# A spiking feed-forward layer with routed experts: ScalarE's bound check on x moved behind the third group's GELU, and more warming products in TensorE's waits

## Chip, cores, metric

The kernel runs on one NeuronCore of a Trainium2 chip. The metric is the device time of one execution in microseconds (us); lower is better. Engines are called PE (TensorE, with PEld for its weight loads), DVE (VectorE), ACT (ScalarE), POOL (GpSimd) and SP (SyncE).

## What is computed

```python
# x: (32, 64, 256) f32, cond: (32, 256) f32, router_w (8, 256), w1 (8, 256, 1024), w2 (8, 1024, 256)
rates  = relu(x) * 0.001
c      = cond[:, None, :] + cumsum(rates, axis=1)
spikes = (floor(c) - floor(c one step before)) / 0.001         # mostly zero
probs  = softmax(spikes.reshape(2048, 256) @ router_w.T)       # 8 experts
top_v, top_i = top_k(probs, 2);  top_v /= sum(top_v)           # capacity 640 slots an expert
for k in range(2):                                              # expert e of token t, if it fits
    out[t] += top_v[t, k] * (gelu(spikes[t] @ w1[e]) @ w2[e])
result = x + out
```

## The kernel before

The kernel counts on few spikes: at most 256 rows of the 2,048 have one, and each has a single spiking channel. It first runs through x, then works out a short list of active rows, routes them, fetches for each row and expert the one row of w1 that its spike picks, and adds the few changed rows to the output. If one of these assumptions fails, a verdict at the end starts a slow general path that does not run here.

**First stage (about 4.7 to 16 us).** x comes in eight groups of 128 x 512. For each, ACT and DVE split the rates in two terms, PE sums them over time (L543, L546, L551), and the floors go through PE once more (L562).

**The middle (16 to 31 us).** It is one chain of small steps that hop between PE, DVE, ACT and POOL: find the spikes, list the rows, compute logits (L621), choose two experts (L1023), rank (L630), drop what exceeds capacity (`limit` L860, `limit_c` L1029, `kept` L1032, `routed` L1033), place (L638 to L649), make one-hot lanes (`ev_lane`, L1044) and, in `make_map(d)` (L662), the list of w1 rows for each of four groups d of two experts. `make_index(d)` writes `w1_index`, and POOL's indirect DMA (L501) gathers 128 rows of w1 into `w1_got`.

**The groups (31 to 56 us).** For each group d: `hidden(d)` (L687) is 8 f32 products, in two halves of four; `gelu(d)` on ACT (L846) takes each half as it is ready; `project(d)` (L703) is 16 products on half the array's columns each; `take_y` (DVE, L1061) and `round_y` (ACT, L877) read the result; `combine(d)` (L713 to L720) adds it to the output rows. PE's order is written out by hand: hidden 0, project 0, take_pairs (L674), hidden 1, hidden 2, project 1, combine 0, hidden 3, project 2, combine 1, project 3, combine 2, combine 3, verdict.

**Warming products.** `keep_warm(n)` issues n matmuls of 512 bf16 columns (L532) whose result nobody reads. They stand in PE's own queue, ahead of the matmuls that come next, so one that is still running when the next input arrives delays it. Six places in the middle take `WARM_MID[0..5]` of them: behind the last `weigh`; behind the event offsets (L589); behind the list and level products (L595 to L603); behind the logits (L621); behind the ranks (L630, L632); behind the places (L638 to L649). Four more, one behind each `make_map(d)`, take `WARM[d]`; the last stands right ahead of `hidden(0)`.

**The check of x.** ACT reads all of x once (128 x 4096), with a bound subtracted, and accumulates whatever is above into column 0 of `faults` (L871); `x_seen` tells DVE. It stands between a dummy activation that loads the GELU table (L867) and `gelu(0)`. DVE waits for `x_seen` ahead of `take_y(1)` and reduces `faults` to one number behind `rest_y(1)` (L1146, L1147), which the verdict matmul at the very end needs.

```python
WARM = (3, 3, 3, 3)
WARM_MID = (2, 2, 2, 1, 1, 2)
```

Of the kernel before, what the change touches and what calls it, by code (L numbers as in the profile page):

```python
# [12 lines left out]
ACT = mybir.ActivationFunctionType  # L13
# [12 lines left out]
def adaln_ffn_kernel(nc, x, cond, router_w, w1, w2, out):  # L26
    B, T, H = x.shape
    E, _, FFN = w1.shape
    N = B * T
    TILES = N // P  # L30
# [16 lines left out]
    FINE = 2.0 ** -17  # L47
    X_MAX = RUN_MAX / (T * float(DT)) - 0.05
    WARM_START = 8
    WARM = (3, 3, 3, 3)  # L50
    WARM_MID = (2, 2, 2, 1, 1, 2)
    XG = TILES // 2
    SIGN_GROUPS = (1, 3, 5, 6)
    PLAIN_GROUPS = tuple(g for g in range(XG) if g not in SIGN_GROUPS)
# [8 lines left out]
    with ExitStack() as ctx:  # L63
        def sb(name, shape, dt=F32):
            return ctx.enter_context(nc.sbuf_tensor(name, shape, dt))
# [4 lines left out]
        def sem(name):  # L70
            return ctx.enter_context(nc.semaphore(name))
# [38 lines left out]
        x_sb = sb("x_sb", [P, TILES, H])  # L110
# [8 lines left out]
        x_bound = sb("x_bound", [P, 1])  # L119
        x_over = sb("x_over", [P, TILES, H], BF16)  # L120
# [72 lines left out]
        faults = sb("faults", [P, NV])  # L193
# [48 lines left out]
        x_in = [sem(f"x_in{i}") for i in range(XG)]  # L242
        w2_in = [sem(f"w2_in{i}") for i in range(E)]
        copied = sem("copied")
        vec = sem("vec")
# [9 lines left out]
        x_seen = sem("x_seen")  # L255
# [272 lines left out]
        def _(pe):  # L528
            def keep_warm(n):

                for _ in range(n):
                    nc.tensor.matmul(bank[2][:, 0:4 * P], ones_b[:, :],  # L532
                                     ones_b[:, :].unsqueeze(1).to_broadcast([P, 4, P]), start=True, stop=True)
# [22 lines left out]
            def weigh(g):  # L556

                wait_floors(pe, g)
                part = zone_half if g in SIGN_GROUPS else zone
                for i in range(2):  # L560
                    at = B - 2 - BPT * (2 * g + i)
                    mm = nc.tensor.matmul(q4_ps, part[:, at:at + P], floors[:, g % RING, i, :],  # L562
                                          start=False, stop=(g == XG - 1 and i == 1))
                mm.then_inc(weighed, 1)
# [18 lines left out]
            weigh(XG - 1)  # L583
            keep_warm(WARM_MID[0])

            pe.wait_ge(masks, MASKS)
            pe.wait_ge(events_set, 1)
            for i, at in enumerate((offset_ps, end_ps)):
                nc.tensor.matmul(at, tri[B:2 * B, i, :, :], events[B:2 * B, :], start=True, stop=True).then_inc(offsets, 1)  # L589
            keep_warm(WARM_MID[1])  # L590

# [12 lines left out]
            mm.then_inc(fetched_more, 1)  # L604
            keep_warm(WARM_MID[2])

# [16 lines left out]
            mm.then_inc(logits, 1)  # L623
            keep_warm(WARM_MID[3])

# [8 lines left out]

            keep_warm(WARM_MID[4])
            pe.wait_ge(routes, 1)
# [13 lines left out]
            mm.then_inc(placed2, 1)  # L650
            keep_warm(WARM_MID[5])

            def make_map(d):

                n = 0
                if d == 0:
                    pe.wait_ge(channels_set, 1)
                    pe.wait_ge(pairs_set, 1)
                for e in (2 * d, 2 * d + 1):
                    pe.wait_ge(maps_set, e + 1)  # L660
                    for t in range(ST):
                        mm = nc.tensor.matmul(MAP[d], ev_lane[:, t, e, :], ev_info[:, t, e, :],  # L662
                                              start=(n == 0), stop=(n == 2 * ST - 1))
                        n += 1
                mm.then_inc(mapped, 1)
# [12 lines left out]
            def hidden(d):  # L678

                pe.wait_ge(w1_in[d], 16)  # L680
                pe.wait_ge(map_out, d + 1)
                for half in range(2):
                    if d >= 2:
                        pe.wait_ge(h_done, 2 * (d - 2) + half + 1)
                    for i in range(CH):
                        f = half * CH + i
                        mm = nc.tensor.matmul(HID[d % 2][half][:, i * PAIRS:(i + 1) * PAIRS],  # L687
                                              w1_got[:, d, f * P:(f + 1) * P], ev_pair[:, d, :], start=True, stop=True)
                    mm.then_inc(h_ready, 1)
# [33 lines left out]
            for d in range(D):  # L723
                make_map(d)
                keep_warm(WARM[d])
            hidden(0)
# [61 lines left out]
        def _(act):  # L788
# [19 lines left out]
            def sign_floors(g):  # L808
                act.wait_ge(cums, g + 1)
                if g >= RING:  # L810
# [23 lines left out]
                                 accum_out=events[B:2 * B, 0:1]).then_inc(events_set, 1)  # L834
# [4 lines left out]
                                 bias=offset[B:2 * B, :]).then_inc(positions_set, 1)  # L839
            clear_got(1)  # L840
            def gelu(d):
                if d >= 2:
                    act.wait_ge(y_ready, d - 1)
                for half in range(2):
                    act.wait_ge(h_ready, 2 * d + half + 1)
                    nc.scalar.activation(hT[:, d % 2, half * CH:(half + 1) * CH, :].rearrange("p f n -> p (f n)"),  # L846
                                         HID[d % 2][half][:, 0:CH * PAIRS], ACT.Gelu, scale=SPIKE).then_inc(h_done, 1)
# [11 lines left out]
            for t in range(ST):  # L859
                nc.scalar.activation(limit[:, t, :], first_two[:, :], ACT.Identity, scale=inactive[:, t:t + 1],  # L860
                                     bias=room_left[:, t:t + 1]).then_inc(limit_set, 1)
# [4 lines left out]
            act.wait_ge(warmed, 1)  # L866
            nc.scalar.activation(warm[:, 2:3], warm[:, 0:1], ACT.Gelu).then_inc(warmed, 1)  # L867

            for g in range(XG):
                act.wait_ge(x_in[g], 16)  # L870
            nc.scalar.activation(x_over[:, :, :].rearrange("p j c -> p (j c)"), x_sb[:, :, :].rearrange("p j c -> p (j c)"),  # L871
                                 ACT.Relu, bias=x_bound[:, 0:1], accum_out=faults[:, 0:1]).then_inc(x_seen, 1)
            def round_y(d):
                act.wait_ge(y_set, d + 1)
                if d >= 2:
                    act.wait_ge(combined, ST * (d - 1))
                nc.scalar.copy(y_hi[:, d % 2, :], y[:, d % 2, :]).then_inc(y_hi_set, 1)  # L877

            for d in range(D):
                gelu(d)  # L880
                if d >= 1:
                    round_y(d - 1)

            act.wait_ge(verdict_set, 1)
            with act.If(act.value_load(verdict[0:1, 0:1]) != P * NV):
# [13 lines left out]
        def _(dve):  # L899
            v = nc.vector  # L900
            steps = [0]

            def link(ins):

                steps[0] += 1
                ins.then_inc(vec, 1)
                dve.wait_ge(vec, steps[0])
# [148 lines left out]
            def take_y(d):  # L1056

                dve.wait_ge(y_ready, d + 1)
                if d >= 2:
                    dve.wait_ge(combined, ST * (d - 1))  # L1060
                v.tensor_scalar(y[:, d % 2, :], Y[d % 2], pair_gate[:, d:d + 1], None, ALU.mult).then_inc(y_set, 1)  # L1061

            def rest_y(d):
                dve.wait_ge(y_hi_set, d + 1)
                v.tensor_tensor(y_lo[:, d % 2, :], y[:, d % 2, :], y_hi[:, d % 2, :], ALU.subtract).then_inc(y_lo_set, 1)
# [73 lines left out]
                                         lead[:, :].unsqueeze(2).to_broadcast([P, ST, TOP_K]), ALU.add, ALU.mult))  # L1139
            C += ST * TOP_K  # L1140
            assert C == NV
            dve.wait_ge(x_seen, 1)
            dve.wait_ge(vec, steps[0])
            take_y(1)
            rest_y(1)
            link(v.tensor_scalar(fine[:, :], faults[:, :], 0.0, None, ALU.is_le))  # L1146
            v.tensor_reduce(fine_sum[:, :], fine[:, :], AX_X, ALU.add).then_inc(summed_up, 1)  # L1147
            take_y(2)
            rest_y(2)
            take_y(3)  # L1150
            dve.wait_ge(rows_in, 16 * ST)
            for t in range(ST):
# [116 lines left out]
```

## Time and profile before

| | |
|---|---|
| runs (us) | 64.33, 64.66, 65.98; median 64.66 |
| the profiled execution (us) | 64.45 |
| its span, first to last instruction (us) | 62.7 |
| PE busy | 52.0 us, 83% |
| DVE busy | 35.5 us, 57% |
| ACT busy | 27.6 us, 44% |
| POOL busy | 19.7 us, 31% |
| mean granted PE clock | 0.892 of 2.4 GHz |

Times in all views count from the span's start; the execution's own time is about 1.75 us more than the span. The durations of matmuls in the records include the run through the array, so that two that overlap add up to more than the time they take; distances between starts show the pace. PE's busy share includes the warming products.

### The profile page before, as it was taken

The page shows a single profiled execution, that of the slowest core. Times are in us where ns is not written, and L with a number is a line of the kernel's source. Part 1 is how long each engine was busy: PE and PEld are TensorE (multiplying, and loading weights), DVE is VectorE, ACT ScalarE, POOL GpSimd, SP SyncE. Part 2 cuts the span into 40 slices and gives each one's busy share as a digit, 9 for nine tenths or more (in the row PEclk, how much of TensorE's full clock was granted, in tenths as well). Part 3 has the DMA queues.
Part 4 walks back from the last instruction along what each step waited for, and adds up shares of the span by engine and source line. Part 5 has one row for each costly group of instructions (what it writes and reads, how often), then busy time and mean ns, then how long its engine had stood idle before and what let it go on. Part 6 is the DMA issues. An engine that isn't in the chain of part 4 may idle for free.

```text
span 62.7 us, 1165 instructions
## 1 busy us (share of the span) xinstructions
PE 52.0 (83%) x376; PEld 30.4 (48%) x376; DVE 35.5 (57%) x158; ACT 27.6 (44%) x46; POOL 19.7 (31%) x59
## 2 busy tenths in 40 slices
PE   3999999997639979999499999999999999990000
PEld 1325456553302614333395589966886576560000
DVE  3389998993687866899899039570330050143000
ACT  0499667944564796099982105830251020000000
POOL 6799893700020620157888000000000000003800
PEclk9999999999985555558999999999999999999955
DMA  0499999999999997114798517999999997000210
GB/s 0 107 361 268 349 342 300 358 339 360 333 349 347 348 349 226 29 18 146 138 342 300 199 28 221 369 282 368 352 349 375 386 387 259 4 0 0 88 60 10
DMA packets 13545, 14.82 MB, mean 236 GB/s; under 512 B 648, under 2 KB 13040, under 8 KB 13536
## 3 DMA queue, kind: packets, MB, share of 16 engines
q1 hardware_dynamic: 12608, 12.62, 61.9%
q0 software_dynamic: 816, 2.01, 10.4%
q8 instruction: 5, 0.08, 0.6%
q10 hardware_dynamic: 112, 0.07, 0.5%
q14 instruction: 4, 0.03, 0.2%
HBM read 13.08 MB, written 2.36 MB: 246 GB/s over the span
## 4 chain that ended last, share of the span: by engine, by line
PE 64%; DVE 11%; issue 7%; DMA 7%; POOL 4%; ACT 2%; POOLq 0%; DVEq 0%
PE bank L703 23%; PE bank L687 12%; PE bank L532 10%; DMA w_got<-in_L_ffn_w_dram,w_index 7%; PE bank L546 4%; POOL out_dram L520 3%; PE bank L551 3%; PE bank L543 3%; PE bank L562 2%; PE bank L719 2%; DVE floors L952 1%; PE bank L720 1%; ACT limit L860 1%; PE bank L713 1%; DVE x_lo L943 1%
## 5 line engine op out<-in xcount | busy, mean ns | idle before, releaser
L532 PE MATMUL bank<-ones_b 128*128 128x512 bf16 x37 | 14.4, 520 | 1.1 <-POOL ones_b L420 1.1
L703 PE MATMUL bank<-w_sb,spare_sb 128*64 128x256 f32 x128 | 14.9, 383 | 0.0
L703 PEld LDWEIGHTS bank<-w_sb,spare_sb 128*64 128x64 f32 x128 | 8.7, 137 | 4.9 <-issue 0.5
L520 POOL DMA_INDIRECT out_dram<-floors,out_index x2 | 2.0, 1019 | 23.1 <-DVE floors L1154 22.8
L687 PE MATMUL bank<-ev_pair,w_got 128*128 128x128 f32 x64 | 7.8, 278 | 0.9 <-DMA w_got<-in_L_ffn_w_dram,w_index 0.9
L687 PEld LDWEIGHTS bank<-ev_pair,w_got 128*128 128x128 f32 x64 | 7.4, 192 | 1.4 <-DMA w_got<-in_L_ffn_w_dram,w_index 1.4
L846 ACT ACTIVATE spare_sb<-bank 128x512 f32<-128x512 f32 x8 | 4.7, 594 | 6.3 <-PE bank L687 6.2
L1061 DVE TENSOR_SCALAR rate<-bank,pair_gate 128x256 f32<-128x256 f32 x4 | 1.9, 485 | 9.5 <-PE bank L703 9.5
L501 POOL DMA_INDIRECT w_got<-in_L_ffn_w_dram,w_index x4 | 4.1, 1023 | 5.5 <-DVE w_index L1050 4.9
L532 PEld LDWEIGHTS bank<-ones_b 128*128 128x128 bf16 x37 | 3.5, 113 | 4.7 <-issue 2.9
L943 DVE SCALAR_TENSOR_TENSOR x_lo<-x_sb,x_hi 128x512 fp32r<-128x512 f32 x8 | 5.4, 687 | 0.1
L805 ACT ACTIVATE x_hi<-x_sb 128x512 fp32r<-128x512 f32 x8 | 4.7, 624 | 0.6 <-DMA x_sb<-in_x_dram 0.5
L877 ACT CAST y_hi<-rate 128x256 fp32r<-128x256 f32 x3 | 1.2, 402 | 7.2 <-DVE rate L1061 7.2
L794 ACT COPY w_got<-zero 128x1024 f32<-128x1024 f32 x4 | 4.1, 1038 | 0.0
L543 PE MATMUL bank<-x_hi,cum_r 128*128 128x512 f32 x8 | 4.0, 494 | 0.0
L871 ACT ACTIVATE x_over<-x_sb,x_bound 128x4096 bf16<-128x4096 f32 x1 | 3.7, 3692 | 0.0
L546 PE MATMUL bank<-x_lo,cum_r 128*128 128x512 f32 x8 | 3.5, 440 | 0.1
L812 ACT ACTIVATE floors<-bank,above 128x512 bf16<-128x512 f32 x4 | 2.7, 687 | 1.8 <-PE bank L551 1.8
L952 DVE TENSOR_SCALAR floors<-bank 128x512 bf16<-128x512 f32 x4 | 2.8, 689 | 1.3 <-PE bank L551 1.2
L551 PE MATMUL bank<-theta,spread 96*128 96x256 bf16 x16 | 3.1, 279 | 0.0
L1044 DVE TENSOR_SCALAR ev_lane<-slot,event_at 128x128 bf16<-128x128 bf16 x16 | 3.1, 249 | 0.0
L1110 DVE TENSOR_SCALAR pair_map<-slot,ev_info 128x64 bf16<-128x64 bf16 x16 | 2.5, 261 | 0.0
(217 smaller groups left out, 76.9 us busy)
## 6 DMA issues: line engine op xcount, KB each, us to landing
w_sb<-in_L_ffn_w_dram SPq DMA_DIRECT2D x8, 1024.0 KB, 11.1
x_sb<-in_x_dram SPq DMA_DIRECT2D x8, 256.0 KB, 4.8
out_dram<-x_sb SPq DMA_DIRECT2D x1, 2048.0 KB, 14.0
cond<-in_cond_dram ACTq DMA_DIRECT2D x2, 32.0 KB, 2.2
w_got<-in_L_ffn_w_dram,w_index POOLq DMA_INDIRECT x4
cond<-in_cond_dram SPq DMA_DIRECT2D x1, 32.0 KB, 2.0
x_rows<-in_x_dram,out_index POOLq DMA_INDIRECT x2
out_dram<-floors,out_index POOLq DMA_INDIRECT x2, 3.1
```

The costliest lines, as they stand in the source:

```text
L501: g.indirect_dma_start(out=w1_got[:, d, :], out_offset=None, in_=w1_rows[:, :], in_offset=bass.IndirectOffsetOnAxis(ap=w1_index[:, d:d + 1 ...
L520: g.indirect_dma_start(out=out_rows[:, :], out_offset=bass.IndirectOffsetOnAxis(ap=out_index[:, t:t + 1], axis=0), in_=ffn_out[:, t, :], i ...
L532: nc.tensor.matmul(bank[2][:, 0:4 * P], ones_b[:, :], ones_b[:, :].unsqueeze(1).to_broadcast([P, 4, P]), start=True, stop=True)
L543: nc.tensor.matmul(CUM[g % 4][:, 0:GW], cum_r[:, :], x_hi[:, g % RING, :, :].rearrange("p j c -> p (j c)"), start=True, stop=False)
L546: nc.tensor.matmul(CUM[g % 4][:, 0:GW], cum_r[:, :], x_lo[:, g % RING, :, :].rearrange("p j c -> p (j c)"), start=False, stop=False)
L551: mm = nc.tensor.matmul(CUM[g % 4][:, i * H:(i + 1) * H], spread[:, BPT * j:BPT * (j + 1), :].rearrange("k b t -> k (b t)"), theta3[:, :], ...
L687: mm = nc.tensor.matmul(HID[d % 2][half][:, i * PAIRS:(i + 1) * PAIRS], w1_got[:, d, f * P:(f + 1) * P], ev_pair[:, d, :], start=True, sto ...
L703: mm = nc.tensor.matmul(Y[d % 2][at, :], hT[:, d % 2, f, at], w2_sb[:, 2 * d + side, f, :], start=(f == 0), stop=(f == FC - 1))
L794: nc.scalar.copy(w1_got[:, d, :], zero1[:, 0:1].to_broadcast([P, FFN])).then_inc(cleared, 1)
L805: nc.scalar.activation(x_hi[:, g % RING, :, :].rearrange("p j c -> p (j c)"), x_sb[:, 2 * g:2 * g + 2, :].rearrange("p j c -> p (j c)"), A ...
L846: nc.scalar.activation(hT[:, d % 2, half * CH:(half + 1) * CH, :].rearrange("p f n -> p (f n)"), HID[d % 2][half][:, 0:CH * PAIRS], ACT.Ge ...
L943: v.scalar_tensor_tensor(x_lo[:, g % RING, :, :].rearrange("p j c -> p (j c)"), x_sb[:, 2 * g:2 * g + 2, :].rearrange("p j c -> p (j c)"), ...
```

## The change

Three things are edited. The numbers of warming products go up at all ten places: in the middle from 10 to 20, behind the maps from 12 to 18. ACT's check of x goes from ahead of `gelu(0)` to behind `gelu(2)` and `round_y(1)`, so ahead of `gelu(3)`. On DVE the wait for it and the two small reductions go from around `take_y(1)` to behind `rest_y(2)`. No DMA is added or moved.

```diff
-    WARM = (3, 3, 3, 3)
-    WARM_MID = (2, 2, 2, 1, 1, 2)
+    WARM = (4, 4, 4, 6)
+    WARM_MID = (3, 6, 3, 3, 2, 3)
@@ scalar
-            for g in range(XG):
-                act.wait_ge(x_in[g], 16)
-            nc.scalar.activation(x_over[:, :, :].rearrange("p j c -> p (j c)"), x_sb[:, :, :].rearrange("p j c -> p (j c)"),
-                                 ACT.Relu, bias=x_bound[:, 0:1], accum_out=faults[:, 0:1]).then_inc(x_seen, 1)
...
+            def check_x():
+                for g in range(XG):
+                    act.wait_ge(x_in[g], 16)
+                nc.scalar.activation(x_over[:, :, :].rearrange("p j c -> p (j c)"), x_sb[:, :, :].rearrange("p j c -> p (j c)"),
+                                     ACT.Relu, bias=x_bound[:, 0:1], accum_out=faults[:, 0:1]).then_inc(x_seen, 1)
+
             for d in range(D):
                 gelu(d)
                 if d >= 1:
                     round_y(d - 1)
+                if d == 2:
+                    check_x()
@@ vector
-            dve.wait_ge(x_seen, 1)
-            dve.wait_ge(vec, steps[0])
             take_y(1)
             rest_y(1)
+            dve.wait_ge(vec, steps[0])
+            take_y(2)
+            rest_y(2)
+            dve.wait_ge(x_seen, 1)
             link(v.tensor_scalar(fine[:, :], faults[:, :], 0.0, None, ALU.is_le))
             v.tensor_reduce(fine_sum[:, :], fine[:, :], AX_X, ALU.add).then_inc(summed_up, 1)
-            take_y(2)
-            rest_y(2)
             take_y(3)
```

## Rows read from the trace of the kernel before

**Rows 1.** Windows: a stretch, its length, busy us by engine, PEclk, DMA, GB/s

```profile
16.00:18.40 2.40, 1.54 (x10) 0.55 (x8) 1.79 (x8) 1.50 (x5) 0.00 (x0) 1.00 1.10 338
18.40:21.90 3.50, 2.85 (x28) 1.40 (x28) 2.97 (x15) 2.31 (x5) 1.28 (x3) 0.51 1.09 348
21.90:25.30 3.40, 3.05 (x31) 1.09 (x28) 2.17 (x14) 2.57 (x4) 0.48 (x2) 0.50 0.88 276
25.30:28.70 3.40, 3.37 (x16) 1.25 (x15) 3.23 (x24) 1.93 (x4) 1.43 (x2) 0.50 0.15 27
```

**Rows 2.** Lines L532 and L662, matmuls at either clock: duration ns min/median/max

```profile
L532 PE MATMUL bank<-ones_b x3: 587/634/634, 25.0 to 25.8; 128*128 128x512 bf16 x3
...
L532 PE MATMUL bank<-ones_b x4: 377/378/380, 28.7 to 29.5; 128*128 128x512 bf16 x4
...
L662 PE MATMUL bank<-ev_info,ev_lane x4: 166/166/213, 26.2 to 26.4; 128*128 128x3 bf16 x4
...
L662 PE MATMUL bank<-ev_info,ev_lane x4: 164/164/168, 29.0 to 29.0; 128*128 128x3 bf16 x4
```

**Rows 3.** Chain of waits that ended last, 18 to 31 us: start, us, what

```profile
22.01 0.70 ACT limit L860 x2
...
24.00 0.87 PE bank L532 x2
...
26.40 4.09 DMA w_got<-in_L_ffn_w_dram,w_index
```

**Rows 4.** Timeline of PE, the middle: start, us, engine line op, [idle before]

```profile
17.27 0.60 PE L532 MATMUL bank<-ones_b 128*128 128x512 bf16 x2
18.89 0.21 PE L595 MATMUL bank<-lists,batch_of 64*128 64x33 bf16 x2 [1.01 <-DVE batch_of L992]
...
19.57 1.03 PE L532 MATMUL bank<-ones_b 128*128 128x512 bf16 x2
20.40 0.85 PE L610 MATMUL bank<-ident_b,spikes 128*128 128x128 bf16 x4
...
21.90 0.59 PE L532 MATMUL bank<-ones_b 128*128 128x512 bf16 x1
22.70 0.20 PE L630 MATMUL bank<-chosen,lead_cum 128*128 128x16 bf16 x2 [0.21 <-DVE chosen L1023]
...
22.78 0.59 PE L532 MATMUL bank<-ones_b 128*128 128x512 bf16 x1
23.49 0.19 PE L638 MATMUL bank<-routed,cum_tile 128*128 128x8 bf16 x1
...
23.86 1.01 PE L532 MATMUL bank<-ones_b 128*128 128x512 bf16 x2
24.68 0.22 PE L662 MATMUL bank<-ev_info,ev_lane 128*128 128x3 bf16 x2
```

**Rows 5.** Timeline of all engines: the lanes, the last products, first `hidden`, last `project`

```profile
24.12 0.74 DVE L1044 TENSOR_SCALAR ev_lane<-slot,event_at 128x128 bf16<-128x128 bf16 x4
...
29.06 0.81 PE L532 MATMUL bank<-ones_b 128*128 128x512 bf16 x3
...
30.75 1.49 PE L687 MATMUL bank<-ev_pair,w_got 128*128 128x128 f32 x11 [0.89 <-DMA w_got<-in_L_ffn_w_dram,w_index]
...
50.94 3.67 PE L703 MATMUL bank<-w_sb,spare_sb 128*64 128x256 f32 x32
```

**Rows 6.** Timeline of ACT: the check, the first GELU's halves, round_y(1), the fourth GELU

```profile
28.36 3.69 ACT L871 ACTIVATE x_over<-x_sb,x_bound 128x4096 bf16<-128x4096 f32 x1
...
32.06 0.57 ACT L846 ACTIVATE spare_sb<-bank 128x512 f32<-128x512 f32 x1
34.08 0.60 ACT L846 ACTIVATE spare_sb<-bank 128x512 f32<-128x512 f32 x1 [1.44 <-PE bank L687]
...
44.95 0.41 ACT L877 CAST y_hi<-rate 128x256 fp32r<-128x256 f32 x1 [3.64 <-DVE rate L1061]
46.24 1.12 ACT L846 ACTIVATE spare_sb<-bank 128x512 f32<-128x512 f32 x2 [0.89 <-PE bank L687]
```

## The prediction

> **What bounds the kernel now.** I read the chain of waits first, then the windows by stage, then the timelines of PE and ACT around the edits. From 31 us on PE hardly stops: `hidden(0)` starts at 30.75 and the last `project` at 50.94 [rows 5], so whatever moves 30.75 moves the end by as much. What moves 30.75 is the gather of w1 rows: 4.09 us of DMA from 26.40, behind an index that the middle produces [rows 3]. The middle itself is a chain of latencies. Its members are mostly DVE and ACT steps (the reader sees `limit`, 0.70 us on ACT, for one); PE is in it through small matmuls and, once, through warming products, 0.87 us from 24.00 [rows 3]. The windows show PE's clock: full (2.4 GHz) up to 18.4, then 0.5 (1.2 GHz) for the three stretches up to 28.7 [rows 1].
>
> **The products, at either clock.** A 512-column product is recorded with 634 ns at half clock and 378 ns at full [rows 2]. The pace is what counts: the three ahead of `hidden(0)`, at full clock, take 0.81 us with a last one of 0.38, so (0.81 - 0.38) / 2 = 0.215 us each [rows 2, 5]; the two from 23.86 at half clock take 1.01 with a last one of 0.63, so 0.38 for a first one, and I take twice 0.215, 0.43, for those behind it [rows 2, 4]. Against that stands the time from where the products start to the next matmul with real input [rows 4, 5]:
>
> - behind the offsets, 17.27 to 18.89: 1.62 us. Six products: 1.29 full, 2.58 half.
> - behind the lists, 19.57 to 20.40: 0.83. Three: 0.65 full, 1.29 half.
> - behind the logits, 21.90 to 22.70: 0.80. Three: 0.65 full, 1.29 half.
> - behind the ranks, 22.78 to 23.49: 0.71. Two: 0.43 full, 0.86 half.
> - behind the places, 23.86 to 24.68, but the last lane that this map needs ends at 24.12 + 0.74 = 24.86 [rows 5], so 1.00. Three: 0.65 full, 1.29 half.
> - ahead of `hidden(0)`, 29.06 to 30.75: 1.69. Six: 1.29 full, 2.58 half.
>
> At full clock each fits, with 0.15 us to spare in the tightest. At half clock the four between 19.6 and 24.9 overrun by 0.46, 0.49, 0.15 and 0.29: 1.39 us on the path to the index. Behind the last `weigh` two products become three while the clock is full in any case; the three behind each of `make_map` 0 to 2 become four, 0.86 us against the 0.74 us of lanes of the next map plus the index steps beside them: no cost at full clock.
>
> **Does the clock stay up?** It fell at 18.4 behind a stretch in which PE, by distances, worked 4 x 0.215 us on products (two of them from 17.27) and little else in the 2.4 us from 16.0 [rows 1, 4]. The change puts seven and more of them there instead of four, 0.215 us each, until 18.56. So I expect no fall at 18.4. The thin place is the next one, 18.6 to 21.9: lists, levels and transposes, and three products, 0.65 us, in 3.3 us. That is hardly denser than what let the clock fall before. I hold it slightly likelier than not that the clock survives it.
>
> **What full clock in the middle is worth.** Small matmuls hardly feel the clock: one of three columns takes 166 ns at half and 164 at full [rows 2]. So the chain's gain is only where columns or products stand on it: the transposes (L610, four of 128 columns), partly hidden behind DVE's own steps, and the products from 24.00, which end 0.18 us ahead of the last lane and so give back next to nothing. Bounds: 0, and 0.87, all of the chain's entry for the products; the lanes' end at 24.86 excludes most of it. I take 0.10. The Trainium skill (TensorE: Matmul & The Clock Gate, section "Single matmul latency") puts an 8-column matmul at 189 ns cold and 169 warm; by its estimate 20 ns a hop over some six hops would be 0.12, against 0.01 by my rows. The sum goes by the rows.
>
> **The check.** Before, it holds ACT from 28.36 until the first GELU starts at 32.06 with no idle time between [rows 6]. The first half of `hidden(0)`, eight of its matmul records at 1.49 / 11 = 0.135 each or less, is done by about 30.75 + 1.1 = 31.85 [rows 5]: 0.1 to 0.2 us too early for ACT, and more if the gather comes sooner. PE has the second half to do meanwhile, so of that only about 0.1 reaches `project(0)`. I take 0.10, bounds 0 and 0.2. The second half's GELU then starts at 34.08, 1.44 us idle behind PE L687 [rows 6], although PE's records of `hidden(0)` are over by about 32.8. I can't explain this wait; `project(0)` may lose some 0.2 us to it. If it hangs on ACT's long instruction or on this execution, it goes: 0 to 0.4, I take 0.10.
>
> At its new place the check starts behind `round_y(1)`, at 44.95 + 0.41 = 45.36, and takes 3.69 plus 0.1 for reading the sum, to 49.15 [rows 6]. Queued behind it is the fourth GELU, which before starts at 46.24: it goes to 49.15 to 50.3. Its first half is needed by `project(3)` at 50.94 [rows 5], and is there at 49.75; the cover is `project(2)` on PE, and 1.2 us of it are left. Each us beyond that would cost one. On DVE `take_y(2)` no longer waits for anything new, and the reductions, under half a us, stand ahead of a `take_y(3)` that waits for PE until about 54.6. Cost: nothing.
>
> **Sum.** 64.45 for the profiled execution, less 0.10 (middle), 0.10 (check) and 0.10 (second GELU): 64.15. That execution lies 0.2 below the median of the three runs, so I add 0.2: 64.35.
>
> **The rivals.**
> - *Clock up throughout* (the forecast): every added product fits its wait. 63.9 to 64.6. Chance 0.50.
> - *The clock falls once, behind the thin stretch, at about 21.9.* Then the products behind logits, ranks and places run at half pace: 0.49 + 0.15 + 0.29 = 0.93 us late, of which the last may be halved because PE is by then nearly always busy, which is how the clock came back at 28.7 before [rows 1]. Less the 0.2 of the check and GELU: 64.66 + 0.3 to + 0.8, 64.9 to 65.4. For it: the thin stretch. Against it: three more products just ahead. Chance 0.27. The Trainium skill (same page, "A second HAM failure mode: psum-queue depth-cycling") describes this case: small idle gaps between groups of matmuls that make the clock go up and down. By it the time would be this rival's.
> - *Slower by over 2%: the clock is down as early as before.* Then the products are a pure load: 1.39 us late at the index, and if half clock lasts until 29, the six ahead of `hidden(0)` overrun by 2.58 - 1.69 = 0.89 instead of being covered; 65.8 to 66.5. It decides from about 1.3 us on, that is, if all four places of the middle are at half pace. Against it: seven products and more where four stood ahead of 18.4. Chance 0.08, of which 0.05 over 2%.
> - *The change does not do what it says*: the clock rises but nothing on the chain depends on it, and the check was never in the way: 64.5 to 64.7. For it: 166 against 164 ns. Chance 0.10.
> - *The check stalls the fourth group* in spite of 1.2 us of cover: chance 0.02. The rest, 0.03, is a gain of over 2% that I don't see, for instance if the profiled execution hides half clocks in later stages that others have.
>
> **How the numbers follow.** The likeliest is 64.35. The range must take in most of the second rival, whose middle is 65.15, and run-to-run spread below: 63.8 to 65.3. By the 2% that a measurement of this kernel can tell from none, faster means below about 63.4: 0.03. Slower means above about 65.95: 0.07, from the third rival and the tail of the second. The same: 0.90.
>
> **What would show it.** Right: PEclk 1.0 in every window from 5 to 56 us; the index of the first map 0.1 us earlier, `hidden(0)` at 30.5 to 30.7; first GELU less than 0.35 us behind its four products; check at about 45.2 with no idle time of PE ahead of the last `project`. Wrong: half clock anywhere between 18 and 29 with L610, L630, L638 or L662 starting directly behind a product, with no idle time before; or idle time of PE in front of `project(3)` put down to ACT L846; or `hidden(0)` that starts right behind the six products.

## The result: slower by 2%, and where the time went

| | median (us) | range | runs |
|---|---|---|---|
| before | 64.57 | 64.22 to 65.98 | 6 |
| changed | 65.96 | 65.46 to 66.08 | 6 |

The ratio is 1.0209, with a 95% interval of 1.0162 to 1.0256: slower, clear of the noise, though whether by 2% it does not say. Medians here and below are of all runs of a kernel, ratios of those within 1.5% of its fastest, so the two can differ by up to 0.8%. The forecast was 64.35, in a range of 63.8 to 65.3; the measured time lies outside it, and on the other side of the median before. The profiled executions are 66.0 (span 64.3) after and 64.45 (span 62.7) before: 1.6 us to be found.

The middle did what was forecast. Windows of the changed kernel, with columns as in [rows 1]:

```profile
16.20:18.60 2.40, 2.28 (x15) 1.03 (x13) 1.81 (x8) 1.51 (x5) 0.00 (x0) 1.00 1.09 347
18.60:22.10 3.50, 2.79 (x31) 1.31 (x30) 2.87 (x15) 2.34 (x6) 1.31 (x3) 1.00 1.10 348
22.10:25.30 3.20, 3.09 (x31) 1.22 (x29) 2.11 (x13) 2.46 (x4) 0.45 (x2) 1.00 0.97 302
25.30:28.70 3.40, 2.89 (x20) 1.14 (x18) 3.24 (x23) 1.69 (x3) 1.47 (x2) 1.00 0.14 21
```

The granted clock is full in all four, where three of [rows 1] had half. Now the timeline of PE around `hidden(0)`, answering [rows 5]:

```profile
29.02 1.46 PE L532 MATMUL bank<-ones_b 128*128 128x512 bf16 x6
30.60 2.05 PE L687 MATMUL bank<-ev_pair,w_got 128*128 128x128 f32 x16
32.63 1.95 PE L703 MATMUL bank<-w_sb,spare_sb 128*64 128x256 f32 x16
36.24 1.95 PE L703 MATMUL bank<-w_sb,spare_sb 128*64 128x256 f32 x16 [1.66 <-ACT spare_sb L846]
```

`hidden(0)` starts at 30.60, 0.15 us earlier than before, and `project(0)` at 32.63, 0.10 us earlier. But the second half of `project(0)` starts 3.61 us behind the first, with 1.66 us of idle PE put down to ACT's GELU. Before, it was 32.73 to 34.72, 1.99 us. 3.61 - 1.99 = 1.62: less the 0.10 it makes 1.52, nearly the whole difference, in one place. ACT's timeline there, answering [rows 6]:

```profile
31.93 0.60 ACT L846 ACTIVATE spare_sb<-bank 128x512 f32<-128x512 f32 x1 [3.51 <-PE bank L687]
35.59 0.60 ACT L846 ACTIVATE spare_sb<-bank 128x512 f32<-128x512 f32 x1 [3.06 <-remote]
```

ACT stood idle for 3.06 us ahead of the second GELU half, although PE's records of `hidden(0)` end at 30.60 + 2.05 = 32.65. The semaphore that PE's last product of `hidden(0)` raises (`h_ready`) is recorded at 35.57, 2.9 us behind the end of that product, and ACT starts 0.02 us later; in the groups that follow the record comes 0.01 us behind the product. In the chain of waits the profile has no name for this time:

```profile
32.53 3.04 another core or an unknown queue
```

So PE did the work, ACT was free, and the word that the work was done came late. I call this *lateness*. It was there before, too: in [rows 6] the halves are 2.02 us apart where every later group has 0.9, and the semaphore's record is 1.25 us behind PE's end, of which `project(0)` covered all but 0.2.

From there on the two kernels are the same, 1.5 us apart (the last `project` starts at 52.46, before at 50.94 [rows 5]). The check of x, at its new place:

```profile
46.67 3.71 ACT L878 ACTIVATE x_over<-x_sb,x_bound 128x4096 bf16<-128x4096 f32 x1
50.28 0.18 ACT L878 ACTIVATION_READ_ACCUMULATOR x_over<-x_sb,x_bound 128x1 f32 x1
50.38 1.06 ACT L846 ACTIVATE spare_sb<-bank 128x512 f32<-128x512 f32 x2
```

The fourth GELU ends at 51.44, and `project(3)`, which needs only its first half to start, does so at 52.46 with no idle time that is put down to ACT.

### The profile page after: what moved, and what is told of

Same layout as the page of the kernel before. It is cut to its first block, busy times and chain, and to the rows that moved or that the text cites. A ratio compares the mean times of both kernels' runs of the same rounds, so it can differ in the third digit from the quotient of the medians.

```text
span 64.3 us, 1196 instructions
## 1 busy us (share of the span) xinstructions
PE 53.1 (83%) x392; PEld 31.4 (49%) x392; DVE 35.5 (55%) x158; ACT 27.5 (43%) x46; POOL 19.3 (30%) x59
## 4 chain that ended last, share of the span: by engine, by line
PE 61%; DVE 10%; DMA 7%; issue 6%; another core or an unknown queue 5%; POOL 4%; ACT 2%; POOLq 0%; DVEq 0%
PE bank L703 20%; PE bank L532 12%; PE bank L687 11%; DMA w_got<-in_L_ffn_w_dram,w_index 7%; PE bank L546 3%; POOL out_dram L520 3%; PE bank L551 3%; PE bank L543 2%; PE bank L562 2%; PE bank L719 2%; ACT spare_sb L846 2%; DVE floors L956 1%; PE bank L720 1%; PE bank L713 1%
## 5 line engine op out<-in xcount | busy, mean ns | idle before, releaser
L532 PE MATMUL bank<-ones_b 128*128 128x512 bf16 x53 | 15.7, 429 | 1.1 <-POOL ones_b L420 1.1
L520 POOL DMA_INDIRECT out_dram<-floors,out_index x2 | 2.0, 1018 | 24.7 <-DVE floors L1158 24.4
L532 PEld LDWEIGHTS bank<-ones_b 128*128 128x128 bf16 x53 | 4.8, 106 | 6.2 <-issue 2.7
```

Of the source, the lines that this page charges most:

```text
L520: g.indirect_dma_start(out=out_rows[:, :], out_offset=bass.IndirectOffsetOnAxis(ap=out_index[:, t:t + 1], axis=0), in_=ffn_out[:, t, :], i ...
L532: nc.tensor.matmul(bank[2][:, 0:4 * P], ones_b[:, :], ones_b[:, :].unsqueeze(1).to_broadcast([P, 4, P]), start=True, stop=True)
```

## How the lateness turns into time

The first half of `project(0)` takes 1.78 us, and the second needs the second GELU half. So the halves of `project(0)` are as far apart as those of the GELU, less 0.02 to 0.14 us, but never less than 1.75 to 1.78. (In the kernels whose GELU halves are 0.7 apart, the check at its old place holds ACT ahead of the first half.) All runs follow this; it is what lets a lateness be read from two starts on ACT. A set is a group of kernels that ran one after another on one chip, beside runs of the kernel before; set 1 is that of the result.

| kernel | set | GELU halves apart (us) | project halves apart (us) | median (us) | before, same set (us) |
|---|---|---|---|---|---|
| before | 1 | 2.02 | 1.99 | 64.57 | |
| changed | 1 | 3.65 | 3.61 | 65.96 | 64.57 |
| e1_warm_only | 2 | 3.48 | 3.46 | 65.98 | 64.66 |
| e2_check_only | 2 | 2.37 | 2.23 | 64.50 | 64.66 |
| e3_gathers_late | 2 | 0.89 | 1.78 | 66.76 | 64.66 |
| e4_tail3 | 2 | 1.63 | 1.78 | 64.34 | 64.66 |
| f1_tail6_alone | 3 | 0.72 | 1.75 | 64.17 | 63.98 |
| f2_tail6_short | 3 | 0.90 | 1.78 | 64.04 | 63.98 |
| f3_rows_late | 3 | 0.90 | 1.78 | 64.03 | 63.98 |
| f4_tail0 | 3 | 0.89 | 1.77 | 64.67 | 63.98 |
| g1_after_again | 4 | 0.89 | 1.78 | 63.91 | 64.29 |
| g2_tail6_alone | 4 | 0.70 | 1.75 | 64.26 | 64.29 |
| g3_rows_late | 4 | 0.89 | 1.78 | 63.80 | 64.29 |
| g4_tail6_short | 4 | 0.89 | 1.77 | 63.95 | 64.29 |
| h1_tail6_alone | 5 | 0.72 | 1.75 | 64.16 | 64.23 |
| h2_rows_late | 5 | 0.89 | 1.78 | 63.93 | 64.23 |
| h3_tail6_short | 5 | 0.89 | 1.78 | 63.81 | 64.23 |
| j1_tail6_alone | 6 | 3.48 | 3.45 | 66.01 | 64.16 |
| j2_rows_late | 7 | 0.89 | 1.77 | 63.85 | 64.12 |
| j3_tail6_short | 7 | 0.89 | 1.77 | 63.94 | 64.12 |

Sets 1, 2 and 6 show the lateness, sets 3, 4, 5 and 7 do not, in any kernel whose trace was kept (of the kernel before, only the trace of set 1 was). There is a second mark that separates them: the trace of every kernel in sets 1, 2 and 6 holds 997 to 1,018 records of semaphore updates, that of every kernel in the others 1,059 to 1,063. Most of the missing ones are landings of POOL's gathers: the landings of the last three gathers of w1 have 16 records each in the sets without the lateness and 4 to 8 in those with it. The updates themselves were not lost: SP's wait for the landing of the third gather ends at 34.55 in the changed kernel of set 1 and at 34.50 in that of set 4. Nor is the traffic another one: in both kernels the gathers' packets start between 28.1 and 36.5 us. It is not the chip's number, for sets 2 and 4 bear the same one.

## Experiments

**One part alone.** *e1* has only the new numbers of products, *e2* only the check's move.

```diff
# e1_warm_only, against the kernel before
-    WARM = (3, 3, 3, 3)
-    WARM_MID = (2, 2, 2, 1, 1, 2)
+    WARM = (4, 4, 4, 6)
+    WARM_MID = (3, 6, 3, 3, 2, 3)
# e2_check_only: the changed kernel with these two lines put back
```

> Only the numbers of warming products are the new ones; the check of x stays ahead of the first GELU. In the changed kernel PE idles 1.8 us in project(0), because the second half of the first GELU starts 3.7 us behind the first instead of 2.0. Theory CHECK (the wait came with the check's move): here it stays near 2.0 us, the time is 64.3 to 64.6. Theory WARM (it came with the products or the clock): here it is near 3.7 us, the time 65.8 to 66.1.

> Only the check of x is moved; the numbers of warming products are the old ones. Theory CHECK: the second half of the first GELU starts about 3.7 us behind the first, the time is 65.8 to 66.1. Theory WARM: about 2.0 us, the time 64.3 to 64.6, and PEclk falls to half between 18 and 29 us as before.

e1: 65.98 us, ratio 1.020 (0.999 to 1.041, wide since four runs only). e2: 64.50, ratio 0.9925 (0.9852 to 0.9998). The timeline of ACT in e1:

```profile
32.42 0.57 ACT L846 ACTIVATE spare_sb<-bank 128x512 f32<-128x512 f32 x1
35.91 0.60 ACT L846 ACTIVATE spare_sb<-bank 128x512 f32<-128x512 f32 x1 [2.91 <-remote]
```

The lateness comes with the products and not with the check. The check's move by itself costs nothing, even in a set with the lateness; whether it gains, the interval, which ends just below 1, hardly says.

**The gathers.** *e3* is the changed kernel with POOL's gathers 1 to 3 of w1 held back until both halves of `hidden(0)` are reported.

```diff
             def gather(d):
+                if d >= 1:
+                    pool.wait_ge(h_ready, 2)
                 pool.wait_ge(cleared, d + 1)
```

> The changed kernel with POOL's gathers 1 to 3 held back until both halves of hidden(0) are reported done. Theory TRAFFIC (the report of the second half of hidden(0) is late because it stands among the gathers' DMA traffic and POOL's descriptor work): the second half of the first GELU starts 0.9 us behind the first, as in every later group. Theory PE (it hangs on what PE has in its queue, whatever the DMAs do): it is still over 2 us behind. The time is worse in either case, by 2 to 5 us, as hidden(1) waits for its rows.

The second half's GELU came 0.89 us behind the first:

```profile
31.63 0.60 ACT L848 ACTIVATE spare_sb<-bank 128x512 f32<-128x512 f32 x1 [3.47 <-PE bank L689]
32.52 0.60 ACT L848 ACTIVATE spare_sb<-bank 128x512 f32<-128x512 f32 x1 [0.30 <-PE bank L689]
```

And the lateness did not vanish; it moved with the gathers. All that POOL has queued behind the first gather, the gathers of x rows too, now moves its data from 35 to 41 us, and a report that falls there is that of `take_pairs` to DVE (all engines' timeline):

```profile
35.92 0.40 PE L676 MATMUL bank<-pair_info,pair_map 128*64 128x4 bf16 x16
...
38.99 0.17 DVE L1121 COPY pairs<-bank 128x16 f32<-128x16 f32 x1 [4.71 <-remote]
```

PE is done at 36.32, DVE starts at 38.99, 2.7 us later; in the kernel before these are 36.90 and 36.95. The reports of the two halves of `hidden(1)`, in the same stretch, are 1.6 and 0.8 us late. So in such a set a report of PE can come late when it falls among the gathers, though not each does: that of `project(0)`, at 36.11 in this trace, is on time. This is one execution, and it does not tell the gathers of w1 from those of x. Nor does it need warming products: none ran within 5 us ahead of `take_pairs`. It is the reading that the other runs are held against.

**The products ahead of `hidden(0)`.** *e4* is the changed kernel with three products there instead of six.

```diff
-    WARM = (4, 4, 4, 6)
+    WARM = (4, 4, 4, 3)
```

> The changed kernel with three instead of six products between make_map(3) and hidden(0). Theory WARM-TAIL (the last six leave PE so busy ahead of hidden(0) that its reports come late): the wait of the first GELU's second half shrinks to 2 us and the time to 64.3 to 64.6. Every other theory: no change, 65.8 to 66.1.

64.34 us, ratio 1.0009 (0.9959 to 1.0059), beside 65.98 for e1 in the same set, where the changed kernel itself did not run:

```profile
31.59 0.60 ACT L846 ACTIVATE spare_sb<-bank 128x512 f32<-128x512 f32 x1 [3.29 <-issue]
33.22 0.60 ACT L846 ACTIVATE spare_sb<-bank 128x512 f32<-128x512 f32 x1 [1.03 <-issue]
```

e4 is 1.6 us faster than e1. The two also differ by the check's place, which e2 puts at 0.2 us by the medians, so three products, 0.65 us of PE time that nobody waits for, are worth about 1.4 us. The lateness shrank from 2.9 to 0.7 us, below the 0.9 that `project(0)` covers.

**The second set of questions, in a set without the lateness.** Four kernels were to tell whether the six products do it alone, by number or by time, and whether the x gathers are part of it.

```diff
# f1_tail6_alone, against the kernel before
-    WARM = (3, 3, 3, 3)
+    WARM = (3, 3, 3, 6)
# f2_tail6_short, against the changed kernel: the last six products
-                                     ones_b[:, :].unsqueeze(1).to_broadcast([P, 4, P]), start=True, stop=True)
+                                     ones_b[:, :].unsqueeze(1).to_broadcast([P, 2, P]), start=True, stop=True)
# f3_rows_late, against the changed kernel
             pool.wait_ge(index_set, 1)
+            pool.wait_ge(pair_mm, 1)
# f4_tail0, against the changed kernel
-    WARM = (4, 4, 4, 6)
+    WARM = (4, 4, 4, 0)
```

> The kernel before with one number changed: six products instead of three between make_map(3) and hidden(0). Theory TAIL (these products alone decide how late the report of hidden(0)'s second half comes): second GELU half 3.3 to 3.7 us behind the first, 65.6 to 66.2. Rival TAIL-WITH-FULL-CLOCK (it takes the full clock through the middle as well): 2.0 to 2.4 us, 64.4 to 64.8.

> The changed kernel with the last six products cut from 512 to 256 columns: as many instructions as in the changed kernel, PE busy as long as with three. Theory COUNT (the number of instructions ahead of hidden(0)): second half 3.3 to 3.7 us behind the first, 65.6 to 66.1. Theory TIME (how lately PE was busy before hidden(0)): 1.6 to 2.0 us, 64.2 to 64.5 as in the run with three.

> The changed kernel with POOL's two gathers of x rows held back until take_pairs is done (about 38 us); the gathers of w1 are left where they are. Theory TRAFFIC-X (the two x gathers are issued at 32.2 and 33.5, just when the report is late): second half 0.9 us behind the first, the time 63.9 to 64.3. Theory TRAFFIC-W (the w1 gathers 1 to 3 are enough): still 3.3 to 3.7 us, 65.6 to 66.1.

> The changed kernel with no product between make_map(3) and hidden(0). If the lateness grows with the products there (0.74 us at three, 2.9 at six), it is gone at none: second half 0.9 us behind the first, 63.6 to 64.3, if the clock stays full over the idle time of 1.5 us; with half clock in hidden(0) 65 and more. If three is already as good as none: 64.2 to 64.5.

All four had the GELU halves 0.7 to 0.9 us apart. Ratios: 0.9951 (0.9898 to 1.0005), 1.0013 (0.9975 to 1.0050), 0.9962 (0.9918 to 1.0007); f4 was 63.74 and 63.95 in two of its runs, with a mean granted clock of 0.98 and 0.97, and 65.4 and 67.15 in the others, with 0.95 and 0.92: too spread for a ratio, and a hint that some products have to stand there. Taken by themselves they would seem to acquit the six products, or to show three cures. The yardstick was missing: the changed kernel itself had not run in this set.

**The yardstick.** *g1* is the changed kernel unaltered; with it ran f1, f2 and f3 again.

> The changed kernel, unaltered, as the yardstick on the chip of this set. On the chip of the first set the report of hidden(0)'s second half came up to 2.9 us late; on the chip of the second set it was not late in any of four kernels, one of which differs from the changed kernel only in POOL's x gathers and one only in the length of six products. Theory CHIP (only some chips show the lateness): either 65.5 to 66.1 with PE idle 1.8 us in project(0) and a second GELU half 3.7 us behind the first, or 63.5 to 64.2 with 0.9 us. Theory KERNEL (the alterations of the second set removed it): 65.5 to 66.1 in any case, with before near 64.0.

> The kernel before with six products ahead of hidden(0), again. If this chip shows the lateness: theory TAIL 3.3 to 3.7 us between the GELU halves and 65.6 to 66.2, its rival 2.0 to 2.4 us and 64.4 to 64.8. If it does not: 0.9 us and within 0.5% of before.

> The changed kernel with the two x gathers held back behind take_pairs, again. If this chip shows the lateness: 0.9 us between the halves and 63.9 to 64.4 by theory TRAFFIC-X, 3.3 to 3.7 us and 65.6 to 66.1 by TRAFFIC-W. If it does not: 0.9 us, equal to the unaltered changed kernel within 0.3 us.

> The changed kernel with its last six products at 256 columns, again. If this chip shows the lateness: theory COUNT 3.3 to 3.7 us between the halves, 65.6 to 66.1; theory TIME 1.6 to 2.0 us, 64.2 to 64.5. If it does not: 0.9 us, equal to the unaltered changed kernel within 0.3 us.

The changed kernel: 63.91 us beside 64.29, ratio 0.9972 (0.9926 to 1.0019). Its GELU halves:

```profile
31.66 0.60 ACT L846 ACTIVATE spare_sb<-bank 128x512 f32<-128x512 f32 x1 [3.28 <-PE bank L687]
32.55 0.60 ACT L846 ACTIVATE spare_sb<-bank 128x512 f32<-128x512 f32 x1 [0.30 <-PE bank L687]
```

Compare these with 31.93 and 35.59 above: the same program, the first starts within 0.3 us, and 3.0 us between the second ones. Theory CHIP stands in so far as the lateness belongs to some sets and not to others. The other three were 1.0019 (0.9975 to 1.0062), 0.9924 (0.9883 to 0.9965) and 0.9923 (0.9875 to 0.9971).

**Two more attempts to meet the lateness.** The three went once more, and then the one that mattered most by itself.

> The kernel before with six products ahead of hidden(0), a third time. In the two sets without the lateness it ran within 0.5% of before. Where the lateness shows: theory TAIL 3.3 to 3.7 us between the GELU halves and 65.6 to 66.2 us; its rival, that the lateness grows with the full clock in the middle too, 2.0 to 2.4 us and 64.4 to 64.8. Where it does not: 0.9 us or less, within 0.5% of before.

> The changed kernel with the two x gathers behind take_pairs, a third time. Where the lateness shows: 0.9 us between the halves and 63.9 to 64.4 by theory TRAFFIC-X, 3.3 to 3.7 us and 65.6 to 66.1 by TRAFFIC-W. Where it does not: 0.9 us, 63.5 to 64.2.

> The changed kernel with its last six products at 256 columns, a third time. Where the lateness shows: theory COUNT 3.3 to 3.7 us between the halves, 65.6 to 66.1; theory TIME 1.6 to 2.0 us, 64.2 to 64.5. Where it does not: 0.9 us, 63.5 to 64.2.

No lateness: 1.0007 (0.9961 to 1.0053), 0.9971 (0.9929 to 1.0013), 0.9919 (0.9875 to 0.9962).

> The kernel before with six products ahead of hidden(0), on yet another chip if there is one. Where the lateness shows: theory TAIL 3.3 to 3.7 us between the GELU halves and 65.6 to 66.2 us; its rival 2.0 to 2.4 us and 64.4 to 64.8. Where it does not: 0.9 us or less, within 0.5% of before.

This set had it. The kernel before with one number changed took 65.97 and 66.06 us beside 63.85 to 64.25 of the kernel before, ratio 1.030 (1.022 to 1.038); first ACT's timeline, then PE's:

```profile
32.24 0.57 ACT L846 ACTIVATE spare_sb<-bank 128x512 f32<-128x512 f32 x1
35.72 0.60 ACT L846 ACTIVATE spare_sb<-bank 128x512 f32<-128x512 f32 x1 [2.90 <-remote]
```

```profile
32.92 1.95 PE L703 MATMUL bank<-w_sb,spare_sb 128*64 128x256 f32 x16
36.37 1.95 PE L703 MATMUL bank<-w_sb,spare_sb 128*64 128x256 f32 x16 [1.51 <-ACT spare_sb L846]
```

Theory TAIL is shown: three more products ahead of `hidden(0)`, with the check at its old place, the old numbers everywhere else and a clock that fell in the middle as before, bring the whole loss where the lateness exists. (Of the 1.85 us, 3.45 - 1.99 = 1.46 are the lateness; another 0.28 is that `hidden(0)` starts at 31.03, where the trace of the kernel before has 30.75, straight behind the last of the six, which ran partly at half clock.) The last two ran in a set without it again:

> The changed kernel with the two x gathers behind take_pairs. Where the lateness shows, as it did in the run just before (66.0 us for six products alone, 64.2 for before): 0.9 us between the GELU halves and 63.9 to 64.4 by theory TRAFFIC-X, 3.3 to 3.7 us and 65.6 to 66.1 by TRAFFIC-W. Where it does not: 0.9 us, 63.5 to 64.2.

> The changed kernel with its last six products at 256 columns. Where the lateness shows: theory COUNT 3.3 to 3.7 us between the halves, 65.6 to 66.1; theory TIME 1.6 to 2.0 us, 64.2 to 64.5. Where it does not: 0.9 us, 63.5 to 64.2.

0.9939 (0.9893 to 0.9985) and 0.9974 (0.9931 to 1.0016), halves 0.89 us apart in both.

**When the late reports come.** The table gives each report of PE in the kept traces that was over half a microsecond late, in us from POOL's issue of the third gather of w1 (29.66 in the kernel before; the later gathers follow it at the same distances in all seven traces). "Due" is the recorded end of PE's product, "came" the semaphore's record. Left out are the first halves of `hidden(0)` in the changed kernel and in e1, late by 0.15 and 0.24 us.

| report | kernel | products just ahead | due | came |
|---|---|---|---|---|
| `hidden(0)`, second half | before | 3 | 3.14 | 4.39 |
| the same | e2_check_only | 3 | 2.89 | 4.37 |
| the same | e4_tail3 | 3 | 2.94 | 3.7 (start of ACT; no record) |
| the same | changed | 6 | 3.03 | 5.94 |
| the same | e1_warm_only | 6 | 2.90 | 5.85 |
| the same | j1_tail6_alone | 6 | 3.13 | 5.85 |
| `take_pairs` | e3_gathers_late | 0 | 1.72 | 4.37 |
| `hidden(1)`, first half | e3_gathers_late | 0 | 4.25 | 5.85 |
| `hidden(1)`, second half | e3_gathers_late | 0 | 5.14 | 5.94 |

This rules out one rival, that six products only shift the report to a worse place among the gathers: it is due at 2.9 to 3.1 with three and with six. And these reports were not delayed by some amount each: all but one came at one of two moments that go with the gathers, about 4.4 or 5.9 us behind the issue, whenever they were due. With three products the report came at the first of these or, in e4, before it; with six it came at the second. Why, no run tells.

**What stays open.** Whether six short products would do as six long ones, and whether holding back the two x gathers would help, since neither ran where the lateness was. What delays the report, and why it comes at the later moment with three more products ahead, is not known: I know only that for `hidden(0)` the 2.7 to 3.0 us took both the gathers in flight and six products just ahead, while `take_pairs` in e3 was 2.6 us late without any. Nor is it known what makes a set late. Since semaphore records are missing from the very same time in the very same sets, the taking of the trace may itself be part of it; every run here was recorded.

## Why the prediction was wrong, point by point

- *What bounds the kernel.* Right. From `hidden(0)` on the loss went to the end one to one.
- *The products at full clock fit their waits.* Right as to their own time: at the lists L610 waits 0.18 us for DVE with three ahead of it, and `hidden(0)` starts at 30.60, 0.1 us behind the end of the six. The tightest place was the logits, as forecast: three products from 21.97 end by their pace at 22.62, and L630 starts at 22.77; it cost nothing, because L638 starts at 23.49 as before.
- *The clock.* The forecast case, at 0.50, came about: full from 6 us to the end of the groups. It seems to have been worth somewhat more than its term of 0.10. `hidden(0)` starts 0.15 us earlier, although this execution reached the middle 0.18 us later (last `weigh` at 16.00 instead of 15.82, in a start where the clock rose at 6.1 instead of 4.8 us): 0.33 us from there to `hidden(0)`, within the term's bounds. Of it 0.22 had been gained when POOL issued the first gather (26.36 instead of 26.40); the rest lies in the gather, not in the middle. The small matmuls gave nearly nothing: the eight-column ones of L621 take a median of 168 ns at half clock before and 166 ns at full clock now, so of the prediction's two prices a hop, 20 ns is not in these rows.
- *The second rival* (0.27: the clock falls once, behind the thin stretch) was no phantom. The kept trace of f3, the changed kernel but for the x gathers, has half clock from 22.3 to 25.5. The last `weigh` starts at 15.89 as in g3, the same kernel with the clock up, and `hidden(0)` at 31.23 instead of 30.45; the time is 64.35 instead of 63.55. That is 0.8 us, the upper end of the rival's 0.3 to 0.8. By the mean granted clock (0.943 to 0.950, where f3's trace has 0.950) 13 of 111 runs with the new numbers in the middle, f4 aside, may have had it. The window of f3, columns as in [rows 1]:

```profile
22.30:25.50 3.20, 3.20 (x28) 1.40 (x27) 1.71 (x10) 2.15 (x3) 0.14 (x1) 0.50 0.75 234
```

- *The check.* Right at both ends. It holds nobody at its new place (start at 46.67, its GELU's first half done at about 50.98, 1.5 us ahead of need, 1.2 forecast). At the old place the first GELU was held 0.14 us past PE's report (32.06 against 31.92), and now it starts 0.02 us behind it; the term was 0.10. Alone the move gave 0.75% in a set with the lateness, with an interval from 0.02% to 1.5%, which does not contradict 0.1 us.
- *The second GELU half.* Here it failed. The prediction saw the 1.44 us [rows 6], said that it could not explain them, and then priced them from one side only, as a gain of 0 to 0.4. A wait without a known cause has no reason to shrink. The term of -0.10 measured +1.62 us. Its cover could have been read from the same rows: `project(0)` had been late by 0.2 us already, so it had no slack left, and each further microsecond of this wait was bound to cost one.
- *The last products.* This is the term put at nothing: the six "fit" their wait of 1.69 us, by PE time alone. Their price was not in PE's time but in a report that ACT waits for, 2 us later. No term of the sum stood for that.
- *The slower rival* had about the right time (65.8 to 66.5, though its own terms, 64.66 + 1.39 + 0.89 - 0.2, reach 66.7) for a wrong reason, half clock; the clock was full. Its 0.05 is no credit to the argument.

In the one set without the lateness in which the changed kernel ran, the forecast was not contradicted: the ratio to before is 0.9972 (0.9926 to 1.0019), and 0.3 us less would be 0.995. So whether the forecast came true hung on the set, which nothing in it foresaw.

Of the versions tried, none is better than the kernel before by 2%. The check's move alone (0.9925) and the changed kernel with three products at the end (1.0009 in a late set, where the six cost 2%) are those that lose nothing where the report comes late; the changed kernel with the x gathers held back is 0.3 to 0.8% faster than before in four sets, none of them late, and in the one set that had both, not to be told from the unaltered changed kernel (0.9924 and 0.9972, with intervals that overlap).

## What to carry to other kernels

A wait in the profile whose releaser had long been done is a term of its own: price it from both sides, look up what covers it, and if the cover is used up, treat anything that could lengthen it as a risk to the whole change. Filler work is not free because its engine is idle; keep it as small as its purpose needs, above all right ahead of a handover to another engine. And run the unaltered kernel in every set of experiments: here a set without it would have acquitted the culprit.

## What the runs showed of the hardware

A semaphore that a matmul raises can reach the waiting engine 2.9 us after the matmul's recorded end (35.57 against 32.66), where 0.01 us is usual in the same trace. In the kept traces such delays happened only while POOL's indirect gathers were moving data and only in three of seven sets. The report of the second half of `hidden(0)` was 2.7 to 3.0 us late with six 512-column products ahead of the group, 1.2 to 1.5 with three and a half-clock middle, 0.7 to 0.8 with three and full clock; with the gathers moved, one of `take_pairs` was 2.6 us late with none. Late reports came 4.37 to 4.39 or 5.85 to 5.94 us behind POOL's issue of the third gather, whenever they were due, but for one at 3.7. The Trainium skill (Perfetto Trace Analysis, section "Per-instruction lifecycle: what the profiler-reported window actually captures") says that the propagation of a semaphore lies outside the window that the profiler reports of an instruction; the trace agrees, since PE's records show nothing of these 2.9 us, and ACT's show them as idle time put down to "remote".
